# Experts' output bias: one 24-row product of split token weights per block inside the open block sums, in place of products and additions token by token

## What is computed

```python
logits = xf @ Wr.T + br
probs = jax.nn.softmax(logits, axis=-1)
top2_prob, top2_idx = jax.lax.top_k(probs, 2)
comb = jnp.zeros((n, e), x.dtype).at[jnp.arange(n)[:, None], top2_idx].add(top2_prob)
h = jax.nn.gelu(jnp.einsum('nd,edh->enh', xf, W1) + b1[:, None, :], approximate=False)
o = jnp.einsum('enh,ehd->end', h, W2) + b2[:, None, :]
y = jnp.einsum('ne,end->nd', comb, o)
```

## Time and profile before

| | us |
|---|---|
| median of 3 runs | 251.25 (250.98 to 252.55) |
| span of the profiled execution | 249.9 |
| PE busy | 230.9 |
| DVE busy | 191.3 |
| ACT busy | 164.2 |
| POOL busy | 62.8 |

### The profile page before, as it was taken

How to read it: one execution, slowest core, us unless ns; L and a number is a source line. 1 busy time by engine, 2 the same in 40 slices (tenths; PEclk the granted TensorE clock), 3 DMA queues, 4 the chain that set the end, 5 groups by cost and what they waited for, 6 DMA issues and landing times.

```text
span 249.9 us, 6298 instructions
## 1 busy us (share of the span) xinstructions
PE 230.9 (92%) x2316; PEld 194.7 (78%) x2316; DVE 191.3 (77%) x481; ACT 164.2 (66%) x509; POOL 62.8 (25%) x94
## 2 busy tenths in 40 slices
PE   1999999999998889989989999999899999999993
PEld 1945665899776766658778899889799999999972
DVE  1576789865668899998186738678999989989991
ACT  2461469752199899993026987422799888898870
POOL 8814132096005465469112400000000000000000
PEclk9999999999999999999999999999999999999999
DMA  6980000000003326064000000069888510001011
GB/s 147 335 217 3 1 0 1 3 3 0 3 0 81 91 65 108 4 212 129 3 7 3 0 3 0 8 103 131 151 211 260 173 37 10 22 4 32 0 42 34
DMA packets 15625, 16.46 MB, mean 66 GB/s; under 512 B 1747, under 2 KB 14367, under 8 KB 15468
## 3 DMA queue, kind: packets, MB, share of 16 engines
q1 hardware_dynamic: 14424, 15.59, 26.0%
q0 software_dynamic: 544, 0.35, 0.6%
q10 hardware_dynamic: 628, 0.14, 0.3%
HBM read 13.91 MB, written 2.16 MB: 64 GB/s over the span
## 4 chain that ended last, share of the span: by engine, by line
PE 54%; DVE 13%; issue 11%; POOL 11%; DMA 4%; ACT 3%; SPq 2%; DVEq 0%; POOLq 0%
PE banks L1328 49%; POOL region_e L471 5%; DMA region_d<-in_L_tok_W_sw 4%; DVE KT L1286 2%; POOL w_lo L526 2%; DVE top L1028 1%; DVE stb L992 1%; POOL region_d L478 1%; PE banks L1531 1%; POOL rstd L413 1%; PE banks L1672 1%; DVE stb L911 1%; ACT region_d L701 1%; DVE y_lo L1269 1%; DVE stats L890 1%
## 5 line engine op out<-in xcount | busy, mean ns | idle before, releaser
L760 ACT ACTIVATE w_sb<-banks,vecs 128x416 f32<-128x416 f32 x60 | 36.4, 608 | 11.2 <-PE banks L1328 8.9
L677 ACT ACTIVATE region_e<-banks,ntop 128x64 f32<-128x64 f32 x128 | 38.3, 346 | 5.0 <-DVE ntop L1035 4.8
L768 ACT ACTIVATE y_hi<-w_sb 128x416 fp32r<-128x416 f32 x60 | 32.7, 548 | 8.1 <-DVE w_sb L1260 8.1
L1269 DVE TENSOR_TENSOR y_lo<-w_sb,y_hi 128x416 fp32r<-128x416 f32 x60 | 34.9, 585 | 1.0 <-ACT y_hi L768 1.0
L677 ACT ACTIVATION_READ_ACCUMULATOR region_e<-banks,ntop 128x1 f32 x128 | 29.8, 238 | 0.0
L1328 PE MATMUL banks<-x_hi,w_hi 128*128 128x416 f32 x80 | 29.3, 366 | 0.0
L1328 PE MATMUL banks<-x_lo,w_hi 128*128 128x416 f32 x80 | 28.1, 352 | 0.0
L1328 PE MATMUL banks<-x_hi,w_lo 128*128 128x416 f32 x80 | 28.0, 350 | 0.0
L1260 DVE TENSOR_TENSOR w_sb<-w_sb,region_c 128x416 f32<-128x416 f32 x40 | 23.4, 586 | 2.5 <-ACT w_sb L760 1.0
L1328 PE MATMUL banks<-y_hi,w_hi 128*128 128x416 f32 x60 | 22.3, 371 | 1.5 <-DVE KT L1286 1.0
L1328 PE MATMUL banks<-y_hi,w_lo 128*128 128x416 f32 x60 | 21.1, 351 | 0.0
(11 more groups left out here) (238 smaller groups left out, 502.1 us busy)
## 6 DMA issues: line engine op xcount, KB each, us to landing
region_c<-out SPq DMA_DIRECT2D x4, 832.0 KB, 14.3
xnT<-out SPq DMA_DIRECT2D x5, 208.0 KB, 13.7
QT<-out SPq DMA_DIRECT2D x5, 208.0 KB, 14.1
region_a<-in_x SPq DMA_DIRECT2D x2, 512.0 KB, 5.3
region_a<-in_x SPq DMA_DIRECT2D x1, 1024.0 KB, 9.5
out<-h SPq DMA_DIRECT2D x2, 512.0 KB, 5.8
h<-out SPq DMA_DIRECT2D x4, 256.0 KB, 5.0
w_sb<-in_L_ffn_W SPq DMA_DIRECT2D x1, 1024.0 KB, 5.6
```

The lines of the kernel that those rows point to most:

```text
L677: last = a.activation(dst[:, h // 2, h % 2], src[:, h // 2, h % 2], ACT.Exp, scale=SCALE, bias=ntop[:, o + h:o + h + 1], accum_out=esum[:, ...
L760: a.activation(lifted(u), bank[h_bank(i)][:, 0:FB], ACT.Gelu, bias=vecs[:, b:b + 1])\
L768: a.activation(h_hi(u), lifted(u), ACT.Copy).then_inc(S["hi_ok"], 1)
L1269: v.tensor_tensor(h_lo(u), lifted(u), h_hi(u).bitcast(F32), ALU.subtract).then_inc(S["lo_ok"], 1)
```

## The change

The bias product moves into the block sums. down_sum of the last expert of a block gets one more matmul, which accumulates b2r (24 rows by 128) times share(blk) (24 rows by 416 tokens) before the sum is closed. The 24 rows are three times eight experts. POOL makes b2r: the rounded b2, its remainder, and the rounded b2 again (with the new constant column K_NM as a mask); and it widens comb to the rounded weights twice and their remainder once, so that the 24-row product stands for the three products of the split operands.

The widened comb is transposed by the four transposes that were there. Rows 8 to 31 of combT are then written to scratch by five more DMAs of SP, behind the broadcasts of block 0, and read back as one [24, 2080] transfer (crow, into the part of region_d that expert 0 leaves), issued ahead of block 2's broadcasts after waits for the writes (d_cs) and for expert 0's products (y2_ps). POOL copies it block by block into three rotating buffers with rounding (share). PE's transposes now wait for POOL (cs_ok) where they waited for DVE's comb_ok.

base on PE and on DVE is gone with its PSUM buffers. up(3, 0), down(0, 4) and down(1, 0) follow up(2, 0) directly; DVE weighs units 0 and 1 after the second group of expert 1 instead of the third, and does rest(0), weigh(2) and rest(1) after the third. The first down_sum waits for expert 1's third group instead of its last. b2 is loaded in three copies instead of four. The last three output DMAs are counted on d_out and SP alone waits for them. Only the parts named here are shown:

```diff
...
+SHARES = 3
...
+        b2r = ctx.enter_context(nc.sbuf_tensor("b2r", [P, C], F32R))
...
+        crow = region_d[0:3 * E, ALL:2 * ALL]
+        shares = ctx.enter_context(nc.sbuf_tensor("shares", [3 * E, SHARES * FB], F32R))
+
+        def share(blk):
+            return shares[:, FB * (blk % SHARES):FB * (blk % SHARES + 1)]
+
+        b2t = y_hi[0:3 * E, 0:C]
+        b2n = tmpx[0:3 * E, 0:C]
...
         def out_expert(e, g):

             n = 5 * e + g
-            return n if n < AHEAD else n + 7
-
-        def out_base(c):
-            return AHEAD + 2 + c
+            return n if n < AHEAD else n + 2
...
             for e in range(DIRECT, E):
                 sp_.dma_start(weights(e)[:, 0:FB], scratch((e - DIRECT) * ALL, [[0, P], [1, FB]]))\
                     .then_inc(S[f"d_we{(2, 3, 4, 4, 6, 6)[e - 2]}"], 16)
+            for c in range(4):
+                sp_.dma_start(scratch((E - DIRECT) * ALL + c * P, [[ALL, 3 * E], [4 * P, 4], [1, P]]),
+                              combT[32 * c + E:32 * c + 4 * E, 0:4 * P].rearrange("e (g m) -> e g m", g=4))\
+                    .then_inc(S["d_cs"], 16)
+            sp_.dma_start(scratch((E - DIRECT) * ALL + TOK, [[ALL, 3 * E], [1, IMG]]),
+                          combT[E:4 * E, 4 * P:4 * P + IMG]).then_inc(S["d_cs"], 16)
             for blk in range(1, 5):
+                if blk == 2:
+                    sp_.wait_ge(S["d_cs"], 16 * 10)
+                    sp_.wait_ge(S["y2_ps"], 5)
+                    sp_.dma_start(crow, scratch((E - DIRECT) * ALL, [[ALL, 3 * E], [1, ALL]]))\
+                        .then_inc(S["d_crow"], 16)
                 b = slice(blk * FB, (blk + 1) * FB)
                 sp_.dma_start(region_c[:, :].rearrange("p (e t) -> p e t", e=4)[:, :, b],
         def _(pool):
             g.dma_start(brb[:, :], br.unsqueeze(0).to_broadcast([P, E])).then_inc(S["d_small"], 16)
-            for c in range(4):
-                g.dma_start(b2s[32 * c:32 * c + E, :], fb2).then_inc(S["d_small"], 16)
+            for c in range(3):
+                g.dma_start(b2s[E * c:E * c + E, :], fb2).then_inc(S["d_small"], 16)
...
+
+            link(g.tensor_copy(b2t, b2s[0:3 * E, :]))
+            link(g.tensor_scalar(b2n, b2t.bitcast(F32), kc[0:3 * E, K_NM:K_NM + 1], None, ALU.mult))
+            g.tensor_tensor(b2r[0:3 * E, :], b2s[0:3 * E, :], b2n, ALU.add).then_inc(S["split_ok"], 1)
+            cb = comb[:, 0:NT, 0:E]
+            pool.wait_ge(S["comb_ok"], 1)
+            link(g.tensor_copy(comb[:, 0:NT, E:3 * E].rearrange("p t (r e) -> p t r e", r=2).bitcast(F32R),
+                               cb.unsqueeze(2).to_broadcast([P, NT, 2, E])))
+            g.tensor_tensor(comb[:, 0:NT, 3 * E:4 * E].bitcast(F32R), cb, comb[:, 0:NT, E:2 * E], ALU.subtract)\
+                .then_inc(S["cs_ok"], 1)
+            pool.wait_ge(S["d_crow"], 16)
+            for blk in range(5):
+                if blk >= SHARES:
+                    pool.wait_ge(S["y3_ps"], 6 * (blk - SHARES) + 6)
+                g.tensor_copy(share(blk), crow[:, blk * FB:(blk + 1) * FB]).then_inc(S["split_ok"], 1)
...
-            accv = KT[:, 0:TOK].rearrange("p (g c d) -> p g c d", g=4, c=4)
-
-            def base(u):
-
-                dve.wait_ge(S["base_ps"], 1 + u // 4)
-                dve.wait_ge(S["acc_ok"], AHEAD)
-                if u < 4:
-                    v.tensor_tensor(accv[:, :, u], bank[out_bank(out_base(u))].rearrange("p (g d) -> p g d", g=4),
-                                    accv[:, :, u], ALU.add).then_inc(S["acc_ok"], 1)
-                else:
-                    v.tensor_tensor(acc[0:IMG, PAIRS, :], bank[out_bank(out_base(u))][0:IMG, 0:C], acc[0:IMG, PAIRS, :],
-                                    ALU.add).then_inc(S["acc_ok"], 1)
...
             for e in range(DIRECT):
                 for g, tiles in enumerate(GROUPS):
                     u = out_expert(e, g)
-                    if (e, g) == (0, AHEAD):
-                        for c in range(5):
-                            base(c)
                     dve.wait_ge(S["y2_ps"], 5 * e + g + 1)
                     if (e, g) == (0, 0):
                         dve.wait_ge(S["comb_ok"], 1)
                     if e > 0:
-                        dve.wait_ge(S["acc_ok"], max(AHEAD + 5, out_done(out_expert(e - 1, tiles[0] // 4))))
-                    elif g >= AHEAD:
-                        dve.wait_ge(S["acc_ok"], AHEAD + 5)
+                        dve.wait_ge(S["acc_ok"], out_done(out_expert(e - 1, g)))
                     for i, t in enumerate(tiles):
                         m = P if t < PAIRS else IMG
                         last = v.scalar_tensor_tensor(acc[0:m, t, :], bank[out_bank(u)][0:m, i * C:(i + 1) * C],
                                                       comb[0:m, t, e:e + 1], acc[0:m, t, :],
                                                       op0=ALU.mult, op1=ALU.add)
                     last.then_inc(S["acc_ok"], 1)
-                    if (e, g) == (1, 2):
+                    if (e, g) == (1, 1):
                         weigh(0)
                         weigh(1)
-                    if (e, g) == (1, 3):
+                    if (e, g) == (1, 2):
+                        rest(0)
                         weigh(2)
-                        rest(0)
+                        rest(1)
                 if e == 0:
                     for c in range(3):
...
             for u in range(3, LATER):
-                if u > 3:
+                if u > 4:
                     rest(u - 3)
                 weigh(u)
...
-            def base(c, g, m=P):
-
-                r = slice(32 * c, 32 * c + E)
-                o = bank[out_bank(out_base(c))][0:m, g * P:(g + 1) * P] if g < 4 else bank[out_bank(out_base(4))][0:m, 0:C]
-                return mm(o, combT[r, g * P:g * P + m], b2s[r, :])
...
-            pe.wait_ge(S["comb_ok"], 1)
+            pe.wait_ge(S["cs_ok"], 1)
             pe.wait_ge(S["acc_ok"], 2)
             for g in range(4):
                 t_.transpose(bank[out_bank(AHEAD)][:, g * P:(g + 1) * P], combP[:, g * P:(g + 1) * P], ident)
...
                 .then_inc(S["cT_ps"], 1)
             down(0, 3)
             up(DIRECT, 0)
-            pe.wait_ge(S["d_small"], 112)
+            up(DIRECT + 1, 0)
+            down(0, 4)
+            down(1, 0)
             pe.wait_ge(S["cT_ok"], 2)
-            pe.wait_ge(S["acc_ok"], AHEAD)
-            for g in range(4):
-                for c in range(4):
-                    last = base(c, g)
-            last.then_inc(S["base_ps"], 1)
-            up(DIRECT + 1, 0)
-            pe.wait_ge(S["acc_ok"], AHEAD + 1)
-            base(0, 4, IMG).then_inc(S["base_ps"], 1)
-            down(0, 4)
-            for g in range(5):
+            for g in range(1, 5):
                 down(1, g)
...
                 if k == 0:
                     pe.wait_ge(S["w2hi_ok"], 1)
                     pe.wait_ge(S["w2lo_ok"], 3)
-                    pe.wait_ge(S["acc_ok"], 15)
+                    pe.wait_ge(S["acc_ok"], out_done(out_expert(1, 2)))
+                    pe.wait_ge(S["split_ok"], 2)
                 if e == DIRECT and blk >= 2:
                     pe.wait_ge(S["at_ok"], blk - 1)
                 o = bank[4 + blk % 2][:, 0:FB]
...
                     w = slice((2 * (e - DIRECT) + s) * C, (2 * (e - DIRECT) + s + 1) * C)
                     mm(o, w2_hi[:, w], h_hi(u), e == DIRECT and s == 0, False)
                     mm(o, w2_lo[:, w], h_hi(u), False, False)
-                    last = mm(o, w2_hi[:, w], h_lo(u), False, e == E - 1 and s == 1)
+                    last = mm(o, w2_hi[:, w], h_lo(u), False, False)
+                if e == E - 1:
+                    pe.wait_ge(S["split_ok"], 3 + blk)
+                    last = mm(o, b2r[0:3 * E, :], share(blk), False, True)
                 last.then_inc(S["y3_ps"], 1)
```

More of the change, by code:

```diff
@@ L47 @@
 K_PM, K_HP, K_KP, K_PR, K_PRIO = 640, 644, 646, 648, 664
-K_ALL = 672
+K_NM = 672
+K_ALL = 673
 V_B1, V_B2, V_SB1, V_SB2, V_BQ, V_BK, V_BV, V_FB1 = 0, 1, 2, 3, 4, 5, 6, 7
@@ L83, in constants @@
     k[:, K_PRIO:K_PRIO + E] = E - np.arange(E)[None, :]
+    k[:, K_NM] = -(p[:, 0] // E == 1).astype(np.float32)
     return k
@@ L235, in scratch @@
             return bass.AP(tensor=out.tensor, offset=out.offset + offset, ap=dims)
-        names = """d_we2 d_we3 d_we4 d_we6 w2hi_ok w2lo_ok d_cs d_wb1 d_wb2 hs_ok hi_ok lo_ok y3_ps at_ok tb_ps fin_ok nm1_ok nmr1_ok xnA_ok d_const d_const2 d_eo d_w1b d_rows d_bias d_w1 d_w2 d_x0 d_x1 d_x2 d_small d_rel d_rvd d_attn d_ffn d_fw1 d_out d_out2 w1hi_ok w1_split
+        names = """d_we2 d_we3 d_we4 d_we6 w2hi_ok w2lo_ok d_cs d_wb1 d_wb2 hs_ok hi_ok lo_ok y3_ps at_ok tb_ps fin_ok nm1_ok nmr1_ok xnA_ok d_const d_const2 d_eo d_w1b d_rows d_bias d_w1 d_w2 d_x0 d_x1 d_x2 d_small d_rel d_rvd d_attn d_ffn d_fw1 d_out w1hi_ok split_ok
         xlo_ok xhi_ok vec_ps vecs_ok eo_act ei_act wn_ok wnT_ps wnT_okA wnT_ok cls_n misc_ps misc_ok nb_ok d_w0
@@ L243, in vit_kernel @@
```

(20 more changed lines are left out.)

## The result

The changed kernel takes 256.06 us (median of 4 runs, 254.95 to 258.15) where the kernel before takes 251.12 us beside it: 1.020 times as long, with a 95% interval of 1.0145 to 1.0263. The sign is as forecast. The size is not: 2.0 us above the 254.1 us forecast and just over the range's end of 256.0 us. Each median in this document is over all runs of a set, and each ratio, with its 95% interval, leaves out the runs more than 1.5% above the fastest of their kernel; the traces of e1_nothing, e4_rows128, e5_own, e7_nowait and e8_direct are of such runs.

A forecast was written before the change was run, and what follows sets the result against it. PE's nearly unbroken chain was taken as the bound, with block 2's DMA landing at 200.8 us as second. Lead 0, landing 2.1 and matmuls 0.76 gave +2.9 us, 254.1 us as median; range 251.5 to 256.0 us.

The forecast's parts named there:

- The sign: Whole kernel: the change makes it slower, +2.9 us; slower by over 1% was given 0.53.
- So a matmul added behind that point costs 0.191 us: PE from 203.01 us, behind block 2's gate: four added 24-row matmuls at the running stream's 0.191 us each, 0.76 us.
- a late copy: POOL's share copies ahead of the added matmuls: not excluded as late for one, seen as a wait; no size given.
- The landing, +2.1 us: DMA queue ahead of block 2's gate: 399,360 added bytes at 191 GB/s make the broadcasts land 2.1 us later.
- the landing hardly moves: Rival, DMA queue: the new rows fill gaps, block 2's gate stays at 200.8 us; 252.0 us, up to 253.5; chance 0.28.
- The lead, 0: DVE's sums run 2.3 us earlier, but wait at the gates of blocks 1 and 2; contribution to the end 0.
- SP's wait, 0: SP waits for the writes ahead of block 2, until near 177.4 us; block 1's transfers cover it, nothing charged.
- SP's five issues: SP's queue: the five writes, issued ahead of block 1's three broadcasts, take 0.33 us each, 1.6 us.
- bubble or few engines: Rival, DMA queue: late issue or few engines cost 3.2 to 5.4 us instead of 2.1; 255.2 to 257.4 us; chance 0.15.
- its bubble: Half of that rival: SP issues the broadcasts of blocks 2 to 4 too late, 5.4 us.
- its few engines: Other half of that rival: the 24 rows lie on few DMA engines; on eight of them the 2.1 us double.
- POOL's widening, 0: POOL's copy and subtraction ahead of the transposes end at 157.1 us, 1.5 us to spare; nothing charged.

The follow-up runs named there:

- e1_nothing: The changed kernel without the whole new bias product (no widened comb, 24-row transfers, copies or added matmuls): 251.2 us, 0.989 of the kernel before.
- e4_rows128: The changed kernel with both operands of the added matmul filled with zeros to 128 rows: 254.66 us, 1.0096 of the kernel before.
- e5_own: The changed kernel with a semaphore of its own for each of blocks 2, 3 and 4: 256.87 us, 1.0138 of the kernel before.
- e7_nowait: The changed kernel without share copies and added matmuls, its read taking 24 other rows so SP need not wait: 255.14 us, 1.0133 of the kernel before.
- e8_direct: The changed kernel with the 24 rows copied from combT to crow inside SBUF, without scratch or SP's wait: 259.77 us, 1.0238 of the kernel before.
- e3_matmuls: The changed kernel without the 24-row writes, read and their waits, keeping copies and added matmuls: 253.53 us, 1.0062 of the kernel before.
- e12_after: The changed kernel as it is, run once more: 255.53 us, 1.0107 of the kernel before.
- e2: The changed kernel without share copies and added matmuls, keeping the widened comb, the transfers and SP's wait: 253.39 us, 1.0086 of the kernel before.
- e9_own128: The changed kernel with 128-row operands of the added matmul and own semaphores for blocks 2 to 4: 252.96 us, 1.0025 of the kernel before.

## Why the prediction was right and wrong

*The failed step: "So a matmul added behind that point costs 0.191 us", four of them 0.76 us.* They cost 0.57 us three times and 0.37 us the last time, 2.1 us by the chain's pieces; the stretch behind weigh(24) is longer by 1.99 us in after, 2.01 in e3_matmuls and 2.23 in e12_after. The 0.191 us was a row of full-row matmuls among their like, taken for an operation that no row showed. On the upper side the step left room only for a late copy, which would be seen as a wait. None was late: PE stays unbroken, as said, but its pitch does not. The trace of before had a hint, outside the rows ahead of the prediction, in two products of 8 rows among full-row ones:

```profile
164.86 0.35 PE L1328 MATMUL banks<-x_lo,w_hi 128*128 128x416 f32 x1
165.15 0.40 PE L1328 MATMUL banks<-b2s,comb_all 8*32 8x128 f32 x2
165.48 8.52 PE L1328 MATMUL banks<-w_all,region_d 128*32 128x128 f32 x72
```

The first of them starts 0.29 us behind the matmul before it, where the stream's step is 0.19. With 2.0 us for 0.76, the forecast's own sum gives 255.3 us. What is then left to the median, 0.7 us, is less than the runs' spread.

*The landing, +2.1 us: the size fits, by luck.* weigh(24) waited for a DMA, at 203.17 us, inside the 202 to 204 us named, and 1.6 to 2.2 us is the mean over the traces. But it was worked out as bytes by a rate, and half the bytes (e8_direct) delay as much. In the profiled execution it was 3.0 us (47.92 for 44.90 behind the product), and DVE was not ready before 47.14 us there: 2.2 of the 3.0 would have come without a late landing. The traces in which weigh(24) stood idle for 1.6 us and more (e2, e4, e7, e8) show the landing by itself. The rival "the landing hardly moves" came true in e12_after, so the two are not two kernels' fates but two executions' of one.

*The lead, 0: nearly right.* weigh(12) was ready at 182.31 us (184.79 less 2.48) instead of 185.88, 2.9 us earlier when the 0.7 us of the front are taken off; I had 2.3. Block 1's gate let 0.55 us of it pass; I had 1.3 at most. The rest stood at that gate as named. (The first down_sum, at 172.61 us instead of 176.36, is 3.1 us earlier with the front taken off; 2 to 3.5 were named.)

*SP's wait, 0: right.* SP stood until 175.54 us, near the 177.4 named, and e7_nowait without the wait is no earlier. *SP's five issues were mis-sized:* 1.6 us were named, and they took 5.3 us (165.04 to 170.33). Block 1's broadcasts were issued 4.7 us later behind the product than in before; their last landing moved by 1.0 us (29.3 us behind the product in the nine traces with the transfers, 28.3 in the five without), ahead of block 2's gate. The rival "bubble or few engines" held the measured time in its range, 255.2 to 257.4 us; its bubble is excluded, its few engines are not, and the 1.2 us that the matmuls cost beyond the forecast are in neither.

*POOL's widening, 0: right* (1.4 us ahead of the transposes). *The share copies, 0: right in this kernel only.* The first three took 0.76 us each for 0.65 and lengthened three DVE operations by 0.33 us, covered by the gate. Where the gate was taken away, they cost about 1.1 us (e9_own128). The Trainium skill ("SBUF — State Buffer", section "SBUF: two separate sides") has a DVE operation with two SBUF inputs and a GpSimd operation that reads SBUF exclude each other for a whole instruction. The trace agrees in kind: 0.91 for 0.58 us, a delay for part of the copy, not for its whole length.

*Not in the prediction: the clock.* It named the waits at both gates but not that PE, standing there, may go on at half speed. In the profiled execution it cost nothing, since DVE was ready for weigh(24) at 202.39 us and the DMA landed later. In e5_own and e1_nothing it did cost. The granted clock is known for every run: of the changed kernel's eight runs three had 0.983 to 0.991 and took 256.02 to 256.83 us, and five had 0.995 or more and took 253.03 to 258.15 us. So it may be part of the median, and the kernel is slower than before without it.

## What to carry to other kernels

Price an added instruction by a row of its own shape, and where there is none, let the range hold the cost of changing shape: a matmul with few rows in a stream of full-row ones cost three times a full-row one, and zeros up to 128 rows bought that back (but clear them where no engine on the path is slowed). A gate that hides one cost hides the others behind it too (here copies, clock and lead), so what a repair of the gate brings is only what the next one leaves. Before building a cheaper product, take it out altogether once: here the whole of it was worth 1.1%, and none of the forms tried was measurably faster than before.

## What the runs showed of the hardware

- A 24-row matmul of 416 columns between 128-row ones took 0.57 us of PE's stream, a 128-row one 0.18 to 0.19: neither its weight load nor the next one was hidden.
- Copies of 24x416 with rounding on POOL, 0.76 us each, made three DVE operations beside them take 0.91 instead of 0.58 us. A clear of 128x1248 on POOL, 1.13 us, made five DVE operations of 128x128 take 2.56 instead of 1.41 us (e9_own128).
- With the 24-row transfers in the queue, the DMA engines moved 104 to 165 GB/s between 24 and 27 us behind the product, and 173 to 219 without them, about as busy in both.
- After PE had stood for 1.28 and 0.50 us at a gate, its granted clock fell to half, and a matmul's pitch went from 0.19 to 0.35 us; in another execution of the same kernel (e12_after), with PE standing for 1.66 and 0.50 us, it did not.
